# Exchanging the halves of k in SBUF: the transfers issued by ScalarE on its own DMA queue instead of by SyncE

## What is computed

```python
q, k, v = proj(x, Wq), proj(x, Wk), proj(x, Wv)      # einsum('bsd,ed->bse'), split in heads
scores = einsum('bhqd,bhkd->bhqk', q * min(cond, 4), k) / sqrt(64)   # causal mask, softmax
a = einsum('bsd,ed->bse', attn @ v, Wo)
s = max(|a|, axis=-1) / 127
y = clip(round(a / s), -128, 127) * s
out = x + einsum('bsi,oi->bso', y, ternary(weight)) + bias
```

## Time and profile before

| | |
|---|---|
| time, median of 3 runs | 2128.12 us (2113.1 to 2131.9) |
| profiled execution | 2122.68 us |
| its span in the profile | 2120.6 us, 2.1 us less than its time |
| mean granted clock of TensorE | 0.97 |
| busy share of the span | PE 93%, PE weight loads 81%, DVE 64%, ACT 48%, POOL 43% |
| DMA | 477.83 MB, mean 225 GB/s |

### The profile page before, as it was taken

How to read it: one execution, slowest core, us unless ns; L and a number is a source line. 1 busy time by engine, 2 the same in 40 slices (tenths; PEclk the granted TensorE clock), 3 DMA queues, 4 the chain that set the end, 5 groups by cost and what they waited for, 6 DMA issues and landing times.

```text
span 2120.6 us, 40315 instructions
## 1 busy us (share of the span) xinstructions
PE 1970.7 (93%) x12378; PEld 1718.5 (81%) x12378; DVE 1365.3 (64%) x3331; ACT 1027.0 (48%) x2495; POOL 907.7 (43%) x984
## 2 busy tenths in 40 slices
PE   8999888799998999998998999999986999999998
PEld 6787667789888998987988988998985777777775
DVE  6545664477788777777666688767776545545454
ACT  4443333467677676776666667766775000000000
POOL 1333443244455444455444455444443444444442
PEclk9999999899999999999999999999997999999999
DMA  6899997877767778677577577677663333332322
GB/s 208 333 371 341 348 361 288 290 232 272 260 204 295 257 249 279 220 278 262 190 247 256 210 262 257 220 270 252 241 235 90 124 109 106 101 118 90 119 89 79
DMA packets 165696, 477.83 MB, mean 225 GB/s; under 512 B 12768, under 2 KB 84448, under 8 KB 135776
## 3 DMA queue, kind: packets, MB, share of 16 engines
q1 hardware_dynamic: 165072, 476.11, 64.7%
q10 hardware_dynamic: 528, 0.52, 0.1%
HBM read 331.88 MB, written 111.15 MB: 209 GB/s over the span
## 4 chain that ended last, share of the span: by engine, by line
PE 69%; DMA 11%; DVE 9%; issue 5%; ACT 3%; POOL 1%; SPq 1%; DVEq 0%; ACTq 0%; POOLq 0%
PE proj_ps L209 19%; PE s_ps L571 8%; PE proj_ps L571 8%; DMA k_sw<-k_st 7%; PE t_ps L985 6%; PE o_ps L373 5%; PE o_ps L642 5%; PE t_ps L335 5%; PE o_ps L985 4%; PE s_ps L295 3%; PE s_ps L296 2%; DMA xv_raw<-xT 2%; DVE k_st L276 2%; DVE pt_all L359 1%; DVE q_st L272 1%
## 5 line engine op out<-in xcount | busy, mean ns | idle before, releaser
L209 PE MATMUL proj_ps<-parts 128*128 128x256 f32 x5376 | 775.5, 293 | 6.6 <-DMA parts<-x_scratch 6.6
L209 PEld LDWEIGHTS proj_ps<-parts 128*128 128x128 f32 x5376 | 684.9, 194 | 17.0 <-DVE k_sum L244 6.5
L325 POOL TENSOR_TENSOR prob<-prob,row_inv 128x128 f32<-128x128 f32 (+3 forms) x512 | 372.5, 728 | 644.3 <-DVE row_inv L319 643.3
L313 ACT ACTIVATE prob<-prob,row_min 128x128 f32<-128x128 f32 (+3 forms) x512 | 287.6, 562 | 209.8 <-DVE row_min L307 205.2
L359 DVE TENSOR_TENSOR pt_all<-t_ps,pt_all 128x128 fp32r<-128x128 f32 (+3 forms) x512 | 249.3, 487 | 117.7 <-ACT pt_all L352 117.5
L307 DVE CUSTOM_DVE_ANT_0 prob<-s_ps,mask 128x128 f32<-128x128 f32 (+3 forms) x512 | 247.2, 483 | 44.3 <-PE s_ps L296 20.0
L335 PE MATMUL t_ps<-ident,prob 128*128 128x128 f32 x1280 | 234.3, 282 | 26.9 <-DVE pt_all L359 22.1
L295 PE MATMUL s_ps<-k_sw,q_st 128*128 128x128 f32 (+3 forms) x512 | 172.7, 337 | 75.8 <-DMA k_sw<-k_st 45.9
L627 ACT ACTIVATE yt_q<-t_ps 128x1024 bf16<-128x1024 bf16 x32 | 32.8, 1024 | 426.6 <-PE t_ps L620 426.6
L352 ACT ACTIVATE pt_all<-t_ps 128x128 fp32r<-128x128 f32 (+3 forms) x512 | 217.0, 424 | 15.3 <-PE t_ps L335 13.7
L335 PEld LDWEIGHTS t_ps<-ident,prob 128*128 128x128 f32 x1280 | 153.1, 143 | 53.6 <-issue 28.6
(11 more groups left out here) (124 smaller groups left out, 2796.5 us busy)
## 6 DMA issues: line engine op xcount, KB each, us to landing
parts<-x_scratch SPq DMA_DIRECT2D x224, 1024.0 KB, 7.5
x_scratch<-xv SPq DMA_DIRECT2D x112, 512.0 KB, 5.7
k_sw<-k_st SPq DMA_DIRECT2D x128, 256.0 KB, 4.1
xv_raw<-xT SPq DMA_DIRECT2D x17, 1024.0 KB, 8.8
v_scratch<-v_tmp SPq DMA_DIRECT2D x64, 256.0 KB, 5.2
v_raw<-v_scratch SPq DMA_DIRECT2D x32, 512.0 KB, 3.9
oT_scratch<-o_sum SPq DMA_DIRECT2D x64, 256.0 KB, 3.4
o_raw<-oT_scratch SPq DMA_DIRECT2D x32, 512.0 KB, 4.6
```

Of the source, the lines that this page charges most:

```text
L209: mm = pe.matmul(qk_bank(w, m), wc[w][:, c, wp, k, :], xq[:, c, :, xp, k, :], start=(fresh and k == 0 and i == 0), stop=(k == CH - 1 and i ...
L313: act.activation(prob[u % QT], prob[u % QT], ACT.Exp, bias=row_min[:, u % 4:u % 4 + 1], scale=-1.0, accum_out=row_sum[:, u % 4:u % 4 + 1]) ...
L325: pool.tensor_tensor(prob[u % QT], prob[u % QT], row_inv[:, u % 4:u % 4 + 1].broadcast_to([P, w]), ALU.mult).then_inc(norm_done, 1)
```

## The change

`swap_k` itself stays as it is, with its wait for the low part of k and its two DMAs. It is now called from `act_step`: exchange 1 of `old` behind the evacuation of q's block 1 and ahead of E(3), exchange 0 of `now` behind H(9) and ahead of OL(1). Both calls go from `sp_step`, and the DMAs run on ACT's DMA queue.

```diff
-        def swap_k(sp, it, blk):
-            sp.wait_ge(proj_lo_done, it * NEV + EVAC[K, blk])
+        def swap_k(eng, it, blk):
+            eng.wait_ge(proj_lo_done, it * NEV + EVAC[K, blk])
...
             evacuate(old, Q, 1)
+            if old:
+                swap_k(act, old[0], 1)
             E(3)
...
             H(9)
+            if now:
+                swap_k(act, now[0], 0)
             OL(1)
...
-            if old:
-                swap_k(sp, old[0], 1)
...
                 load_xq(sp, nxt[0], nxt[2], M_P7)
-            if now:
-                swap_k(sp, now[0], 0)
```

More of the change, by code:

```diff
@@ L277, in evac_lo @@
                                       ALU.subtract).then_inc(proj_lo_done, 1)
-        def swap_k(sp, it, blk):
-            sp.wait_ge(proj_lo_done, it * NEV + EVAC[K, blk])
+        def swap_k(eng, it, blk):
+            eng.wait_ge(proj_lo_done, it * NEV + EVAC[K, blk])
             heads = slice(2 * blk, 2 * blk + 2)
-            sp.dma_start(k_sw[0:DH, heads, :].bitcast(F32), k_st[DH:P, heads, :].bitcast(F32)).then_inc(k_swapped[blk], 16)
-            sp.dma_start(k_sw[DH:P, heads, :].bitcast(F32), k_st[0:DH, heads, :].bitcast(F32)).then_inc(k_swapped[blk], 16)
+            eng.dma_start(k_sw[0:DH, heads, :].bitcast(F32), k_st[DH:P, heads, :].bitcast(F32)).then_inc(k_swapped[blk], 16)
+            eng.dma_start(k_sw[DH:P, heads, :].bitcast(F32), k_st[0:DH, heads, :].bitcast(F32)).then_inc(k_swapped[blk], 16)
         def scores(pe, it, u):
```

## The result

| | before | after |
|---|---|---|
| time, median | 2129.28 us, 4 runs (2113.1 to 2131.9) | 2211.2 us, 4 runs (2207.48 to 2216.28) |
| ratio, 95% interval | | 1.0403 [1.0347, 1.0459] |
| span of the profiled execution | 2120.6 us | 2205.7 us |

The forecast was 2137 us, with a range up to 2166 us. The measured time lies outside it: the kernel is slower by 82 us where 9 were expected (from the median of 2128).

A forecast was written before the change was run, and what follows sets the result against it. PE was taken as the bound, its wait at S(0) for the exchange nearly all it loses. Terms 5 + 10 + 2.5 + 2.4 - 5 = +15 us on 2122.68 gave 2137 us; range 2105 to 2166.

The forecast's parts named there:

- Where S(0) stands: At S(0): the transfer is slow, not its issue; M(14)'s chain ends almost as late, so at most 1.2 us to gain.
- Exchange 0 on ACT: Ahead of OL(1): wait and issues make T(12) 1.2 us late; costs 5 us over 23 passes, 10 us over 8 others.
- Exchange 1 on ACT: Ahead of E(3): hidden under the high part of q in loop passes, 2.5 us; 2.4 us in passes with weight splitting.
- The first step: At the first S(0): ACT's queue avoids seven queued loads; gain 5 us, S(0) at about 388 us.
- The step that failed: the transfer: Exchange 0 on ACT's queue: about 6 us, since P7 goes out before it and P3 right behind it.
- what SyncE gains: On SP: P3 can go out up to 3.2 us earlier, beside exchange 0; worth nothing in itself.
- The estimate of 6.6 us: Exchange 0 beside a load, queues taking turns by packet: 2.9 us on top of 3.7, no gain.
- Rival 2: At S(0): early P3 gets between, exchange 0 lands 1.2 us later in 31 steps; 2165 us, chance 0.19.
- Rival 1: At S(0): issue hardly holds ACT, transfer lands early, 1.2 us less in each of 23 passes; 2090 us, chance 0.18.
- Rival 3: At exchange 0: the queue changes nothing, transfer stays 6.5 us, also in the first step; 2145 us, chance 0.18.

The follow-up runs named there:

- e6: Kernel before, both exchanges on SyncE, with load P7 issued behind exchange 0 instead of ahead of it: 2070.47 us, ratio 0.9746.
- e7: Kernel after, with load P3 moved behind the store of `o_sum` in SyncE's order: 2113.04 us, ratio 0.9925.
- e8: Kernel after, with loads P7 and P3 both moved behind the store of `o_sum`: 2102.98 us, ratio 0.9899.
- e1: Kernel after, with exchange 0 back on SyncE behind P7, so only exchange 1 is on ACT: 2126.09 us, ratio 0.9996.
- e4: Kernel before, with load P3 issued ahead of exchange 0 on SyncE's queue: 2227.88 us, ratio 1.0451.
- e9: Kernel before, with three extra matmuls of constants in the wait of S(0) in each later step: 2131.99 us, ratio 1.0051.
- e5: Kernel after, with three extra matmuls of constants in the wait of S(0) in each later step: 2165.98 us, ratio 1.0193.
- e2: Kernel after, with exchange 1 back on SyncE, so only exchange 0 is on ACT: 2208.69 us, ratio 1.0365.
- e3: Kernel after, with SyncE waiting for the low part of k again, ahead of load P3 only: 2229.48 us, ratio 1.0463.

## Why the prediction was wrong

**Where S(0) stands.** The reading of the kernel before was right: the transfer, not its issue, was late, and two chains ended close together at S(0). "The most that a faster transfer can give here is 1.2 us": e6, in which it is faster, gave 0.8 us in a loop pass, though 57 us in all. In the stage, PE is idle at S(0) for 21.6 us in place of 60.5 and busy for 1097.13 in place of 1114.87: the passes of the kernel before that had waits near 3 us and a low clock gained more.

**Exchange 0 on ACT.** Right in mechanism and nearly in size. The issues took 0.47 and 0.62 us on ACT, in an unbroken row behind DVE's L276; OL(1) started at 877.24, 1.43 us behind the low part of k, where 1.30 was forecast; T(12) waited a median of 0.95 us, where 1.2 was. "PE's time lost is the same as before under another name" holds in e7, where the transfer is as early as in the kernel before: idle at S(0) and T(12) is 33.3 + 28.8 = 62.1 us, against 61.3. What ScalarE's part costs once the transfer no longer covers it is in the difference from e8 to e6: 28.6 of the 32.5 us, 0.9 us in each of 31 steps.

**Exchange 1 on ACT.** Right in the loop passes: ACT's sequencer issued under the high part of q (896.00, while L263 went on to 897.22), E(3) followed without a gap, and e1 equals before. The 4.9 us of the sum for it can't be told from nothing.

**The first step.** Right. S(0) came at 388.18 us, where 388 was forecast, behind a gap of 6.23 us in place of 11.54, and the exchange landed after 8.2 and 10.5 us, not 13.4 and 15.0. The rows are, for PE and for the two transfers of the kernel after:

```profile
388.18 0.45 PE L295 MATMUL s_ps<-k_sw,q_st 128*128 128x128 f32 x1 [6.23 <-issue]
```

```profile
DMA to landing us min/median/max: 8.2/9.3/10.5
```

The other runs bear it out. In the seven kernels with exchange 0 on ACT the gap is 5.9 to 6.9 us and the second transfer lands after 10.2 to 11.2; in the four with it on SyncE behind P7 (before, e1, e4, e9) it is 10.0 to 12.5 us and 13.4 to 15.9. In this one step, with six loads of 1 MB issued in the 8 us before it in the kernel before, a queue of its own did help.

**The step that failed: the transfer.** "I take about 6 us, since the loads don't stop", and, under what SyncE gains, that the earlier P3 "is worth nothing in itself". The second transfer took 9.4 us in the median, 2.8 us more than before. The prediction had noted that P3 could go out up to 3.2 us earlier, and treated it as a neighbour of the exchange when it had become its predecessor. The earlier trace rows already priced it: one load in front made 6.5 us out of 3.7, that is 2.8 us, and a second load in front added the same again. The estimate of 6.6 us, by packets that take turns, missed the same thing: the packets do take turns, but the exchange's first one started only 3.85 us behind its issue, with its own queue empty in front of it. Why it stands still there, no run shows. Rival 2 had the mechanism and its threshold right (over 6.9 us S(0) follows the landing) but took 1.2 us for it, and so came to 2165 us. At 2.8 us late, and with 1.2 us of slack used up, PE idles 66.5 us more in the stage, 2.1 us in each step.

**The term that was missing: the clock.** No term of the sum, and none of the rivals, let PE run slower behind a longer wait. Yet the kernel before showed it: a mean clock of 0.97, and 0.50 in the 4.1 us behind its S(0) at 1043.07, which had waited 2.88 us. The prediction read two windows with the clock at 1.00 and took them for all. Against the kernel before this term is 26 us by the busy time of PE. The whole of what the kernel after loses to its clock is more, 36 us against the busy time in e8, which has the same program but for the loads' places, and 45 us by e5; but part of that is in the 2122.7 us already (9 us, by the busy time in e8). With what was measured in place of both, the sum comes out: 2122.7 + 66.5 (PE idle in the stage) + 26.4 (PE slower) - 5.0 (first step) - 2.9 (behind the stage) = 2207.7 us, and the profiled execution took 2207.48.

**Rivals 1 and 3.** Rival 1 (S(0) follows M(14) as it did) fell by the late transfer and by the wait at T(12). Rival 3, the transfer as late as before, is what e7 makes true: 2145 us was forecast, 2113 measured. It charged 22 us, all in the stage, which grew by only 2.5 us (1197.43 for 1194.93): the idle time at S(0) and T(12) stayed as it was (above), the other idle time of PE grew by 8 us, and the clock of the stage went up from 0.97 to 0.99, with PE's busy time 6 us less (1108.80 for 1114.87). Of the rest, 3.4 us are the first S(0), at 389.82 us, 4.0 stand behind the stage, where the kernels don't differ, and 4.5 are the distance from e7's profiled execution to its median.

## What to carry to other kernels

A wait in a queue holds back everything behind it, and can be what keeps a transfer that matters ahead of bulk loads; before moving such a wait, list what will now be issued ahead of the transfer, and price each load by how much the loads already in front delay it. A transfer that is waited for should be issued before the loads that nobody waits for, on whichever queue; a queue of its own did that here only in the first step. And price a wait of TensorE together with the matmuls behind it: look at the granted clock in the first microseconds after it, in the passes with long waits, not at the mean.

## What was not expected of the hardware

- **Two queues, little preference.** A 256 KB transfer between SBUF tiles, the second of a pair, took 3.7 us alone, 6.6 to 7.1 us with one 1 MB load issued before it, and 9.3 to 9.8 us with two, whether on the loads' own queue (e4) or on another (after, e2), and whether the second load was issued 1.9 us ahead or at the same time (e3). A load issued 3 us later on the other queue (e7) cost it little, 6.7 for 6.6 us, and two loads issued right behind it on its own queue (e6) hardly anything, 3.8 for 3.7. Only in the first step, behind a whole row of queued loads, did the other queue save anything: 10.2 to 11.2 us in place of 13.4 to 15.9.
- **The clock after a wait.** With waits of 0.99 us at T(12) and 2.37 us at S(0), 1.9 us of matmuls between them, TensorE was granted 0.58 of its full clock over the next 4.1 us; behind a single wait of 2.88 us, 0.50; behind the 1.62 us of the earlier trace rows the pass ran at 1.00. The length of the wait alone doesn't decide it: in the kernel before, the clock fell behind two waits of 1.69 us (0.64 and 0.58) and not behind one of 2.77 us. The Trainium skill ("TensorE: Matmul & The Clock Gate", section "HAM oscillation — how this bites in real kernels") describes a kernel in which each wait for a DMA sends the clock down again; the trace of the kernel after agrees, behind 29 of its 31 later S(0), with 19 matmuls in such 4.1 us against 32 in e5.
- **Work in place of idling pays.** In e5 PE was busy for 1184.00 us of the stage in place of 1141.24, with six more matmul instructions in each step, and the stage took 1253.80 us in place of 1287.88.
